# First cross-attention: key tiles taken in pairs on TensorE

## The reference

```python
ci = rms_norm(hidden_states, ln_post_cross_w)
cq = heads(ci @ cq_w, NH, CHD)             # 16 heads of 8 features
ckv = encoder_outputs @ ckv_w
ck, cv = jnp.split(ckv, 2, axis=-1)
ck, cv = (heads(ck, NH, CHD), heads(cv, NH, CHD))
cctx = sdpa(cq, ck, cv, causal=False)      # softmax over 1500 keys
cctx = cctx.transpose(0, 2, 1, 3).reshape(b, l, CC)
hidden_states = hidden_states + cctx @ cdense_w
```

## Time and profile before

| | |
|---|---|
| median of 3 runs | 1500.37 us |
| the profiled execution: its time | 1499.86 us |
| the profiled execution: its span | 1498.1 us, mean granted TensorE clock 0.987 |
| TensorE matmul busy | 1414.9 us (94%), 7850 instructions |
| VectorE | 908.5 us (61%) |
| ScalarE | 583.7 us (39%) |
| GpSimd | 554.1 us (37%) |
| busy in the stage of the change, in tenths of a slice (slices 5 to 15 of 40, 37.5 us each) | TensorE 8 or 9 (7 in the last), VectorE 6 or 7 (0 in the last), ScalarE 4 to 6, GpSimd 4 to 8 |

### The profile page before, as it was taken

How to read it: one execution, slowest core, us unless ns; L and a number is a source line. 1 busy time by engine, 2 the same in 40 slices (tenths; PEclk the granted TensorE clock), 3 DMA queues, 4 the chain that set the end, 5 groups by cost and what they waited for, 6 DMA issues and landing times.

```text
span 1498.1 us, 20649 instructions
## 1 busy us (share of the span) xinstructions
PE 1414.9 (94%) x7850; PEld 738.8 (49%) x7851; DVE 908.5 (61%) x1429; ACT 583.7 (39%) x878; POOL 554.1 (37%) x385
## 2 busy tenths in 40 slices
PE   6979899999999979998989899998999899999998
PEld 3446555555555544445653355554344355555344
DVE  6887766666666607312256688886424678887440
ACT  1263466666666642003433344443133234434131
POOL 1630488888888870000001244450001045542000
PEclk9989999999999999999999999999999999999999
DMA  7001532323232204007550011100032001110000
GB/s 270 1 1 34 148 84 73 89 68 103 55 103 59 57 1 188 0 0 304 200 183 3 12 40 39 39 26 3 1 119 69 0 27 39 47 43 2 2 0 25
DMA packets 45030, 95.73 MB, mean 64 GB/s; under 512 B 6860, under 2 KB 28892, under 8 KB 44908
## 3 DMA queue, kind: packets, MB, share of 16 engines
q1 hardware_dynamic: 44912, 94.21, 20.4%
HBM read 72.04 MB, written 0.97 MB: 49 GB/s over the span
## 4 chain that ended last, share of the span: by engine, by line
PE 84%; DVE 8%; POOL 3%; issue 2%; ACT 2%; DMA 0%; SPq 0%; ACTq 0%; POOLq 0%; DVEq 0%
PE psum L1640 23%; PE psum L2148 10%; PE psum L1881 5%; PE psum L1857 5%; PE psum L1831 4%; PE psum L2089 4%; PE psum L1814 3%; PE psum L2120 3%; PE psum L2140 3%; PE psum L1800 3%; POOL XN L701 3%; PE psum L2143 2%; PE psum L2141 2%; PE psum L2142 2%; DVE WA L1328 2%
## 5 line engine op out<-in xcount | busy, mean ns | idle before, releaser
L1328 DVE TENSOR_REDUCE WA<-psum 112x2 f32<-112x1000 f32 x192 | 229.8, 1200 | 89.9 <-PE psum L1831 89.9
L701 POOL TENSOR_TENSOR XN<-XN,WBZ 125x896 f32<-125x896 f32 x128 | 266.8, 2084 | 16.8 <-POOL XN L701 0.9
L1041 ACT ACTIVATE WA<-psum,y_bias 125x448 f32<-125x448 f32 x192 | 121.2, 634 | 201.8 <-PE psum L2143 200.8
L923 ACT ACTIVATE WBZ<-psum 125x896 f32<-125x896 f32 x192 | 175.5, 915 | 43.9 <-PE psum L1857 33.2
L2148 PE MATMUL psum<-WA,ctxN 125*128 125x448 f32 x384 | 178.7, 548 | 0.9 <-ACT WA L1041 0.7
L732 POOL TENSOR_TENSOR XN<-const,y_max 112x896 bf16<-112x896 f32 x32 | 75.2, 2351 | 263.0 <-DVE y_max L1536 190.7
L1536 DVE CUSTOM_DVE_ANT_0 XA<-psum,WA 112x375 bf16<-112x375 f32 x240 | 125.3, 541 | 46.9 <-PE psum L2120 45.8
L723 POOL TENSOR_SCALAR ctxT<-ctxT 128x375 f32<-128x375 f32 x32 | 56.2, 1756 | 252.4 <-ACT std L796 249.8
L1857 PE MATMUL psum<-R 100*125 100x224 f16 x768 | 110.6, 266 | 0.0
L1549 DVE RECIPROCAL WBZ<-WBZ 128x224 f32<-128x224 f32 x68 | 104.9, 1545 | 0.1
L1857 PEld LDWEIGHTS psum<-R 100*125 100x125 f16 x768 | 78.9, 135 | 28.3 <-issue 25.0
(11 more groups left out here) (254 smaller groups left out, 2344.9 us busy)
## 6 DMA issues: line engine op xcount, KB each, us to landing
R<-WA SPq DMA_DIRECT2D x192, 93.8 KB, 2.2
WA<-in_ctxT SPq DMA_DIRECT2D x14, 750.0 KB, 4.2
ctxT<-in_ctxT SPq DMA_DIRECT2D x11, 750.0 KB, 4.0
ctxN<-in_ctx SPq DMA_DIRECT2D x32, 192.0 KB, 2.5
ctxT<-in_ctxT SPq DMA_DIRECT2D x32, 187.5 KB, 2.4
R<-in_ctx SPq DMA_DIRECT2D x7, 768.0 KB, 8.3
R<-in_ctxT SPq DMA_DIRECT2D x7, 750.0 KB, 6.9
WA<-in_ctx SPq DMA_DIRECT2D x6, 768.0 KB, 6.8
```

Source lines behind the costliest of these rows:

```text
L701: nc.gpsimd.tensor_tensor(z_sum[b % 2][0:TK, :], first[0:TK, :], z_p[t % 4][0:TK, :], ALU.add)\
L923: nc.scalar.activation(z_p[t % 4][0:TK, :].rearrange("p (k n) -> p k n", k=2), psum[0:TK, s:s + 2, 0:2 * GC], ACT.Exp, scale=float(CHD0) * ...
L1041: nc.scalar.activation(y_pT[t][0:TK, g * HALF:(g + 1) * HALF], bank[2 + u % 3][0:TK, 0:HALF], ACT.Exp, bias=y_bias[0:TK, bass.ds(b * NT + ...
L1328: V.tensor_reduce(z_mx[0:PR, r:r + 3:2, c], psum[0:PR, lo:lo + 2, 0:PC], AX_X, ALU.max)\
```

## The change

TensorE's loop takes two tiles at a time. The scores of tiles t + 2 and t + 3 come first, then one unit, the attended values of tile t, those of tile t + 1, after the last pair the three sums, then the second unit, then both halves of a projection. The first scores of a batch and the second are issued in the last pair of the batch before; for batch 0, ahead of the loop. ScalarE and VectorE follow the same order of pairs. On ScalarE the exps of the next batch's first two tiles stand ahead of `evacuate`; on VectorE `invert` stands behind the maxima of tiles 2 and 3, where it stood behind that of tile 3 already, but those two maxima now come in one pair. GpSimd and SyncE are not edited; every product, exp, maximum and add is still there, once.

```diff
-        VALUES_AT = {0: (0, 0), 1: (0, 1), 2: (1, 0), 3: (1, 1), 4: (2, 0), 5: (2, 1)}
-        KEYS_AT = {6: (0, 0), 7: (0, 1), 9: (1, 0), 10: (1, 1), 11: (2, 0), 12: (2, 1)}
+        VALUES_AT = {0: 0, 2: 1, 4: 2}
+        KEYS_AT = {6: 0, 8: 1, 10: 2}
...
@@ ScalarE @@
             exps(0, 0)
+            exps(0, 1)
             for b in range(B):
-                for t in range(NT):
+                for t in range(0, NT, 2):
                     if t == 0 and b > 0:
                         evacuate(b - 1)
...
+                    for u in (t + 2, t + 3):
+                        if u < NT:
+                            exps(b, u)
+                        elif b + 1 < B:
+                            exps(b + 1, u - NT)
+                        if b + 1 < B and t == TURN_AT and u == t + 2:
+                            shifts(b + 1)
+                    if b + 1 < B and t in VALUES_AT:
+                        values(b + 1, VALUES_AT[t])
+                    if b + 2 < B and t in KEYS_AT:
+                        high_keys(b + 2, KEYS_AT[t])
@@ VectorE @@
-                for t in range(NT):
-                    for m, k in ahead(b, t):
+                for t in range(0, NT, 2):
+                    for m, k in ahead(b, t) + ahead(b, t + 1):
                         maximum(m, k)
                         if k == UNITS - 1:
                             combine(m)
...
+                    if b + 2 < B and t in KEYS_AT:
+                        low_keys(b + 2, KEYS_AT[t])
-                    if b > 0 and t == 3:
+                    if b > 0 and t == 2:
                         invert(b - 1)
@@ TensorE @@
+            scores(0, 1)
             for b in range(B):
-                for t in range(NT):
-                    for m, k in ahead(b, t)[0:1]:
+                for t in range(0, NT, 2):
+                    units = ahead(b, t) + ahead(b, t + 1)
+                    for u in (t + 2, t + 3):
+                        if u < NT:
+                            scores(b, u)
+                        elif b + 1 < B:
+                            if b + 1 == EARLY and u == NT:
+                                pe.wait_ge(sem("z_queries1"), STACKED)
+                            scores(b + 1, u - NT)
+                    for m, k in units[0:1]:
                         unit(m, k)
                     if b + 1 < B and t == TURN_AT:
                         turn_maxima(b + 1)
...
                     attended(b, t)
                     if b == B - 1 and t >= COOL:
                         warm(7, 1)
-                sums(b, 0)
-                if b + 2 < B:
-                    keys(b + 2, *KEYS_AT[NT])
-                for i in range(1, ADDED):
-                    sums(b, i)
+                    for m, k in units[1:-1]:
+                        unit(m, k)
+                    attended(b, t + 1)
+                    if b == B - 1 and t + 1 >= COOL:
+                        warm(7, 1)
+                    if t + 2 == NT:
+                        for x in range(ADDED):
+                            sums(b, x)
+                    for m, k in units[1:][-1:]:
+                        unit(m, k)
+                    for side in range(2):
+                        if b + 1 < B and t in VALUES_AT:
+                            values(b + 1, VALUES_AT[t], side)
+                        if b + 2 < B and t in KEYS_AT:
+                            keys(b + 2, KEYS_AT[t], side)
```

More of the change, by code:

```diff
@@ L947, in _ @@
             exps(0, 0)
+            exps(0, 1)
             for b in range(B):
-                for t in range(NT):
+                for t in range(0, NT, 2):
                     if t == 0 and b > 0:
                         evacuate(b - 1)
[L952 to L961, removed]
-                if b + 2 < B:
-                    high_keys(b + 2, PIECES - 1)
+                    for u in (t + 2, t + 3):
[9 more added lines that the diff above has]
+                        high_keys(b + 2, KEYS_AT[t])
             evacuate(B - 1)
@@ L1365, in _ @@
                             combine(m)
-                    if b + 2 < B and t in KEYS_AT and KEYS_AT[t][1] == 1:
-                        low_keys(b + 2, KEYS_AT[t][0])
-                    if b > 0 and t == 3:
+                    if b + 2 < B and t in KEYS_AT:
+                        low_keys(b + 2, KEYS_AT[t])
+                    if b > 0 and t == 2:
                         invert(b - 1)
-                if b + 2 < B:
-                    low_keys(b + 2, PIECES - 1)
             invert(B - 1)
@@ L1929, in _ @@
                         turn_maxima(b + 1)
[L1930 to L1943, removed]
                     attended(b, t)
```

## The result

The changed kernel takes 1519.43 us (median of 4 runs, 1517.47 to 1520.68), the kernel before 1501.07 in the same comparison (4 runs): a ratio of 1.0125, 95% interval 1.0108 to 1.0141. It is 18 us slower. The forecast was 1500.9 with a range to 1507, so the time lies above it.

The account below looks back on a forecast made before the run. TensorE was taken to bound 13 of 15 batch intervals, something else the last two. 13 x 0.01 = 0.1, the 14th interval +1.0 and the opening 0 gave +1.1, hence 1500.9 us, range 1497 to 1507.

Parts of the forecast that it names:

- The slots and the saving of 0.27 a pair: TensorE start-to-start times of product groups; a pair of tiles falls from 3.72 to 3.45 us if nothing waits.
- The chain of 1.71 and unit B's wait: Unit, VectorE's maximum, next unit: at least 1.71 us apart, so a pair's second unit waits 0.45.
- The turn in pair 8: Turned maxima on TensorE at tile 8, between the pair's two units, which then stand 2.05 us apart, or 2.15.
- the sums in pair 10: Sums at tiles 10 and 11 on TensorE put the two units 2.46 us apart, so the second waits for nothing.
- The late reciprocal: VectorE's reciprocal, behind both maxima of pair 2, makes GpSimd's quotient wait 0.7 us.
- The second exp ahead of the emptying: On ScalarE the next batch's second exp, needing add 9, delays the accumulator bank's emptying by 0.3 us.
- the ring: GpSimd's adds and quotient, last sums, emptying, divide: from 23.4 to 24.4 us a batch, deciding only the 14th interval.
- the second rival: Slower: low keys precede the next first unit's maximum on VectorE at full length; +0.90 us a batch, 1512.6; chance 0.15.
- half as long again: Range bound: GpSimd's two delays half as long again give 24.9 us a batch and 1506.3 us in all.
- The opening: Batch 0: first units some 2 us later, two tiles of scores gone before its sums; cost 0, bounds -1 and +1.
- The third rival: TensorE standing still 0.45 us three times a batch drops the clock to 1.2 GHz; tens of microseconds; chance 0.01.
- The faster rival: The second unit hardly waits, the draining saved comes out in full, GpSimd decides at 23.7 us; 1489.8 us; chance 0.07.

Follow-up runs that it names:

- the kernel with half maxima: Kernel with emptying and reciprocal both moved early, without fillers, each maximum over only half of its unit's keys; 1488.28 us in a single execution.
- the real maxima: Kernel with early emptying, early reciprocal and fillers, full maxima, and the second unit between the projection halves in the early pairs only; 1487.92 us, ratio 0.9911.

## Why the prediction was wrong

What TensorE and VectorE do was right, step by step:

- The slots and the saving of 0.27 a pair: a value pair without the wait takes 3.42 and 3.43 (pairs 2 and 4 of the kernel with half maxima) against 3.45 worked out. The Trainium skill, TensorEngine Tiling (Array Packing), section Tiling Modes, says that a change of the tiling mode drains the engine. The trace agrees: where nothing waits, pairs of one form are the cheaper ones, 3.42 against 3.72 before.
- The chain of 1.71 and unit B's wait: A to B is 1.71 in pairs 2, 4 and 6 and 1.80 in pair 0 (forecast 1.71 and 1.81), TensorE idle 0.40 to 0.42 before unit B with the maximum as what ended it (forecast 0.45). The changed kernel in pair 4 (pairs are counted by their first tile); pairs 2 and 6 read the same:

```profile
278.07 0.42 PE L1829 MATMUL psum<-WA,XB 32*112 32x500 f16 x2
278.41 0.96 PE L1879 MATMUL psum<-WBZ,ctxN 125*32 125x224 f32 x16
...
279.78 0.42 PE L1829 MATMUL psum<-WA,XB 32*112 32x500 f16 x2 [0.40 <-DVE WA L1328]
```

- The turn in pair 8: 2.01 (forecast 2.05); the sums in pair 10: 2.37 where no add holds them back (2.46). The whole of TensorE's batch: 24.39, seen with the emptying moved (24.53). Of the 0.14 between them 0.09 is pair 10 and 0.04 pair 8.
- The late reciprocal: the quotient waits 0.59 where the emptying is early (0.7). The second exp ahead of the emptying: 0.3 forecast, and the changed kernel's 14th interval, which has no keys and in which the quotient waits for nothing, is 23.66 against 23.42 without it (0.24). With both delays the 14th measures 24.27 (forecast 24.4).

What failed is the step "ScalarE now takes the second exp ... ahead of the emptying ... 0.3 later". It counted what the change had put ahead of the emptying in the text, and not what stood there already. The high keys of the last pair keep their place on ScalarE, but what they wait for moved on TensorE from before the last sums to behind them. The term was 0.3 and measured 1.88, so the ring is 25.3 and not 24.4 at most, and the 13 intervals cost +10.4 and not +0.1. That is the sign of being wrong that the forecast had named: intervals above 24.8, and GpSimd's add as what ended the wait before the last sums. The number was even there: the second rival says that high keys are ready at S' + 2.0. It was held against VectorE's queue alone, where it does no harm, and never put into ScalarE's. Measured, the copy starts at S + 2.02, behind an exp that ends at S + 0.98 and not near S' + 0.5. The forecast followed the steps that moved on ScalarE, not those whose producer moved on TensorE. The bound of "half as long again" was taken from the two known terms and so could not reach a term that was missing; with it the range ended at 1507.

The opening was costed at 0, with bounds of 1 either way, and measured +4.0: 1.7 is the same missing term once more, and 1.9 the clock, a cost that the sum had put at nothing. The third rival gave the clock 0.01, on the ground that the last batch is emptier than the new order. That holds for the inner batch shown, whose granted clock stayed 1.00 at 22.59 busy of 25.27. It did not look at the first pair of batch 0, where two extra units stand behind each other with the chain's wait between them; the forecast treated batch 0 as one number. The price there was 2 us, not tens.

The faster rival's time was 1489.8, and a kernel in which unit B hardly waits measures 1488.28, with the real maxima 1487.92: its ring figure, 23.7 with a late emptying, is 23.4 with an early one. The slower rival's time of 1512.6 came nearer the result than the forecast, but by a mechanism that isn't there: the low keys put a maximum of unit A back by 0.10, not by their 0.67 (270.14 low keys, 270.74 maximum, where 0.45 behind its unit would be 270.64).

## What to carry to other kernels

For each instruction that closes a ring, list everything that stands ahead of it on its in-order queue, unchanged lines too, and ask of each of them whether what it waits for has moved on another engine; idle time just ahead of that instruction will not show it, since the wait stands ahead of another instruction of the queue. Work that shares one buffer (here the units and their maximum) is best spread at even distances. In this kernel two close and one far costs the wait of the close ones and wastes the slack of the far one. Price the first and the last round of a loop by themselves.

## What the hardware showed beyond that

- The clock fell to its lower level at about 167.3, in a wait of 1.39 us ahead of a unit and after one of 0.78 (TensorE busy 0.83 of the 3 us from 165 to 168). In the kernel with half maxima, which has no fillers, it fell too, at about 165.3, in a wait of 0.87 and after one of 0.26, and was back at about 172.2; in the last batch of the kernel before, with 18.09 busy of 23.40, it stayed up. At the lower level a unit's record is 0.66 long, not 0.42. Three filler products behind each of the two units in the middle kept it up, though the wait of 0.78 was still there (166.32).
- In the last batches the granted clock differed between kernels whose TensorE loops are alike there (0.84 in the changed kernel and 1.00 with the early emptying and reciprocal, both from 545 to 555 us), without changing the intervals, which are the ring's. No run tells why.
- Half a projection costs by what stands on both of its sides: 0.54 between a unit and scores, 0.64 between attended and a unit (267.10 to 267.74 in the kernel with unit B between the halves). Splitting a projection around a unit gives back a part of what the pairs save, 3.62 to 3.68 for a value pair in place of 3.42, and was still the better choice.
